# Graph-attention block on one core: probabilities times normalised tokens, head weights afterwards

## The chip, the core and the metric

The kernel runs on one core of a Trainium2 chip. The metric is the device time of one execution in microseconds, taken as the median of the runs shown. A core has TensorE (PE, matrix products into the accumulators called PSUM), VectorE (DVE), ScalarE (ACT), GpSimd (POOL) and SyncE (SP, which here only issues DMAs), and 16 DMA engines that they share. Each engine works through its own list of instructions in order and meets the others through semaphores.

## The reference, cut to what matters

There are 8 batches of 1024 tokens with 256 features and one adjacency matrix of 1024 x 1024. The first layer is a plain graph layer, the second a graph-attention layer with 4 heads, a second attention with one head over the joined heads, and a feed-forward network.

```python
h = jnp.maximum(_layernorm(x), 0.0)
x = x + deg[None, :, None] * (h @ Wi.T + b) + einsum('ij,bjo->bio', adj, h @ Wj.T)
h = jnp.maximum(_layernorm(x), 0.0)
# attention, for each head: Wh = h @ W[head], a logit for each pair of tokens from two vectors
Wh = jnp.einsum('bnf,hfo->bhno', h, W_heads)
e = f1[:, :, :, None] + f2[:, :, None, :]
e = jnp.where(adj > 0, leaky_relu(e, 0.01), -1e9)
attn = jax.nn.softmax(e, axis=-1)
head = jax.nn.elu(jnp.einsum('bhnm,bhmo->bhno', attn, Wh))
# heads joined: the same attention once more with W_out, elu, then
y = jnp.maximum(out @ w1 + b1, 0.0) @ w2 + b2 + out
x = x + layernorm(y) * gamma + beta
```

For a head, `attn @ (h @ W)` equals `(attn @ h) @ W`.

## The kernel before

Products of float32 quality are made from float16 parts: a value is split into a high and a low part, and three products (high-high, high-low, low-high) are added in PSUM. Such a split is made by ACT for the high part and by DVE for the low part, both reading the same source.

**Units and pairs.** The attention is cut into units of 128 rows of probabilities over 1024 columns. A batch has 32 units in layer 1 (4 heads x 8 row tiles) and 8 in layer 2; the 320 units run in a fixed order (lines 580 to 590): after the start, 32 units of layer 1 of one batch alternate with 8 units of layer 2 of the batch before. Two units are a pair. For each unit DVE adds logits and mask (`masked_row`, L941), ACT applies the leaky slope (L810), the exponential (L816) and the division (L823, `p_hi`), DVE makes `p_lo` (L948), POOL makes the small shift and the inverse of the sum (L742 to L757), and SP issues two transposes by DMA that bring the probabilities into `pt_hi` and `pt_lo` (L706, L708). There are 5 rows of logits (`X_SLOTS`), 2 of probabilities (`P_SLOTS`) and 4 of transposed ones (`T_SLOTS`). `attend` (L1166 to L1192) multiplies a pair by the values: 48 matmuls of 256 columns into psA. In layer 1 the values `val_hi` and `val_lo` are Wh, all four heads, and the result goes through elu (L829, L956, L962), a split (L837, L968) and `project` (L1194 to L1206, 12 matmuls of 258 columns with W_out into psD). After the fourth head of two row tiles ACT and DVE make `valo` (L842, L974) and `f12o` (L976), which are the values and logits of layer 2.

**The order.** Each engine runs one loop over steps n (from `START` to `STOP`); one unit enters per step, and a stage for unit k stands at step k plus its lag. The lags before: logits -5, leaky -4, exponential -3, `p_hi` -2, `p_lo` -1, transposes -1, `attend` +2, `elu_exp` +4, `elu` and `ht_high` +5, `ht_low` +6, `project` +7, `valo` +8. The step is only a position in each engine's list; engines drift apart as far as the semaphores and buffers let them.

**Side work.** Between the stages of the units stand the products that prepare the next batch and finish the one before. Their steps are fixed numbers relative to the first unit of the batch (`front(n, s)`, L645) or to the end of its layer 2 (`end2`): loading x (-46), its statistics and normalisation (-40 to -33), the graph products `z` and `d` (-32 to -27, two products of 16 matmuls of 512 columns each, twice), their eviction into `cat16` (L857, L1022), `x1` (-24 and -22, 48 matmuls of 256 columns each), the addition to xx (L1029), the second normalisation, `h1T` (-17 and -15, transposes on TensorE into PSUM, evicted as h1 by L862 and L1035), score rows (-12), their transpose (-10), storing and loading the logits (`save_f2`, `load_cat`), and `wh` (L1262 to L1267): one row tile of h1 times all four head weights, 12 matmuls of 512 columns, in each of the last 8 steps before the batch; for batch 1 all eight in one step. `wh` is evicted by `val_high` (L875) and `val_low` (L1046). The first pair of a batch waits for all eight (L1173). The feed-forward network (`ff1`, `ff2`, two halves) stands at +0, +2, +4, +6 after layer 2. All side products take turns on two PSUM buffers, psB and psC (`bank_task`, L617 to L625); each waits until the one two places earlier has been evicted (`open_bank`, L1208). `save_f2o` (L767) is a store of 1024 single elements into DRAM, issued by POOL 20 steps before `end2`.

Of the kernel before, what the change touches and what calls it, by code (L numbers as in the profile page):

```python
# [5 lines left out]
ALU = mybir.AluOpType  # L6
# [4 lines left out]
P = 128  # L11
# [9 lines left out]
VAL_SCALE = 2.0 ** (WH_LOG - LN_LOG - W_LOG)  # L21
CAT_LOG = 1
P_LOG = 15
VALO_SCALE = 2.0 ** (6 - WH_LOG - W_LOG)
X_SLOTS = 5
P_SLOTS = 2
T_SLOTS = 4


def build(nc, x, adj, w0, b0, w_heads, a_heads, w_out, a_out, w1, b1, w2, b2, gamma, beta, out):  # L30
# [12 lines left out]
    with ExitStack() as ctx:  # L43
# [44 lines left out]
        ff_half, y_half = big[:, 2, :], (big[:, 3, :], big[:, 0, :])  # L88
        o2T_half = tuple(big[:, i, :].rearrange("p (k n) -> p k n", k=KF) for i in range(2))
# [6 lines left out]
        h1_hi = hs_hi[:, :].rearrange("p (k n) -> p k n", k=KF)  # L96
        h1_lo = hs_lo[:, :].rearrange("p (k n) -> p k n", k=KF)
# [12 lines left out]
        h1hi_done, h1_done = sem("h1hi_done"), sem("h1_done")  # L110
# [23 lines left out]
        def scalar_stages(act, yy):  # L134
# [12 lines left out]
            def h1(s, k):  # L147
                act.wait_ge(h1_ps, s * 2 + k + 1)
                nc.scalar.activation(h1_hi[:, k, :], psD[:, :], ACT.Relu).then_inc(h1hi_done, 1)
            return h0, z_out, h1  # L150

        def vector_stages(dve, yy):
# [56 lines left out]
            def h1(s, k):  # L209
                dve.wait_ge(h1hi_done, s * 2 + k + 1)  # L210
                nc.vector.scalar_tensor_tensor(h1_lo[:, k, :], psD[:, :], 0.0, h1_hi[:, k, :], ALU.max, ALU.subtract).then_inc(h1_done, 1)
            return stats_of, means_of, normalise, h0, add_bias, z_out, x1, stats_x1, stats_x, h1
# [47 lines left out]
        with ExitStack() as tmp:  # L260
# [47 lines left out]
            with nc.Block() as block:  # L308
# [42 lines left out]
                def _(act):  # L351
                    h0, z_out, h1 = scalar_stages(act, yy)
# [19 lines left out]
                    h1(0, 0)  # L372
                    h1(0, 1)

                @block.vector
                def _(dve):
                    stats_of, means_of, normalise, h0, add_bias, z_out, x1, stats_x1, stats_x, h1 = vector_stages(dve, yy)
# [92 lines left out]
                    nc.vector.tensor_scalar(ebits[:, S_HINV:S_HINV + 1], kf[:, 0:1], -float(WH_LOG + P_LOG), None, ALU.add)  # L470
# [11 lines left out]
                    h1(0, 1)  # L482

# [46 lines left out]
        val_hi = sb("val_hi", [P, T, H, F], F16)  # L530
        val_lo = sb("val_lo", [P, T, H, F], F16)
# [20 lines left out]
        rows = yy[0:2 * H, :, :].rearrange("c t f -> c (t f)")  # L552
        stats_y = sb("stats_y", [P, T // 2, 6], F32)
# [14 lines left out]
        f1_done, rows_done, whhi_done, wh_done = sem("f1_done"), sem("rows_done"), sem("whhi_done"), sem("wh_done")  # L568
        x_in, x1_saved = sem("x_in"), sem("x1_saved")
        out_added = [sem(f"out_added_{i}") for i in range(2)]  # L570
        bank_full = [sem("psB_full"), sem("psC_full")]
# [778 lines left out]
```

## Time and profile before

| | |
|---|---|
| median of 3 runs | 1856.02 us (1854.7 to 1857.63) |
| the profiled execution's own time | 1850.8 us |
| its span | 1849.0 us |
| busy: PE / DVE / ACT / POOL | 1649.6 / 1473.5 / 1388.5 / 996.6 us |
| granted TensorE clock, mean | 0.957 |
| DMA, share of 16 engines (SP's queue) | 65.5% |

Busy time is the union of the instructions' durations on an engine. The end of a matmul is modelled and matmuls overlap, so for TensorE the distance between two starts says more than the duration. The granted clock is a share of the full 2.4 GHz.

### The profile page before, as it was taken

The page shows a single profiled execution, that of the slowest core. Times are in us where ns is not written, and L with a number is a line of the kernel's source. Part 1 is how long each engine was busy: PE and PEld are TensorE (multiplying, and loading weights), DVE is VectorE, ACT ScalarE, POOL GpSimd, SP SyncE. Part 2 cuts the span into 40 slices and gives each one's busy share as a digit, 9 for nine tenths or more (in the row PEclk, how much of TensorE's full clock was granted, in tenths as well). Part 3 has the DMA queues.
Part 4 walks back from the last instruction along what each step waited for, and adds up shares of the span by engine and source line. Part 5 has one row for each costly group of instructions (what it writes and reads, how often), then busy time and mean ns, then how long its engine had stood idle before and what let it go on. Part 6 is the DMA issues. An engine that isn't in the chain of part 4 may idle for free.

```text
span 1849.0 us, 34618 instructions
## 1 busy us (share of the span) xinstructions
PE 1649.6 (89%) x12568; PEld 1273.5 (69%) x12568; DVE 1473.5 (80%) x2459; ACT 1388.5 (75%) x1789; POOL 996.6 (54%) x1414
## 2 busy tenths in 40 slices
PE   6679979989999899898998899998998989988865
PEld 4437766678777777687676777677776876867653
DVE  5787876879887887978888798878879788788573
ACT  4078886879868797778886698687977789799560
POOL 2056653546465664746555565655646456586351
PEclk9789999999999999999999999999999999998988
DMA  6056783578757885759955897579856688589562
GB/s 222 25 122 106 138 178 57 109 102 160 157 90 117 132 177 102 110 102 140 176 98 97 119 161 145 91 112 133 176 102 105 104 140 158 101 145 134 101 97 42
DMA packets 713292, 225.57 MB, mean 122 GB/s; under 512 B 678784, under 2 KB 706432, under 8 KB 712992
## 3 DMA queue, kind: packets, MB, share of 16 engines
q1 hardware_dynamic: 704160, 214.92, 65.5%
q0 software_dynamic: 8960, 8.42, 3.9%
q8 instruction: 100, 1.64, 0.4%
q14 instruction: 72, 0.59, 0.1%
HBM read 38.54 MB, written 16.94 MB: 30 GB/s over the span
## 4 chain that ended last, share of the span: by engine, by line
PE 59%; DVE 15%; issue 6%; DMA 6%; ACT 4%; POOL 4%; SPq 1%; DVEq 0%; ACTq 0%; POOLq 0%
PE ps L1163 19%; PE ps L1191 10%; PE ps L1184 10%; PE ps L1185 10%; PE ps L1204 5%; DVE p_lo L948 3%; DMA pt_hi<-p_hi 3%; DVE xr L941 3%; PE ps L1283 2%; DMA pt_lo<-p_lo 2%; ACT xr L810 1%; ACT xr L816 1%; PE ps L1285 1%; ACT p_hi L823 1%; DVE stats_y L1058 1%
## 5 line engine op out<-in xcount | busy, mean ns | idle before, releaser
L1184 PE MATMUL ps<-pt_hi,val_hi 128*128 128x256 f16 x2048 | 474.8, 278 | 46.3 <-DMA pt_hi<-p_hi 27.7
L1185 PE MATMUL ps<-pt_hi,val_lo 128*128 128x256 f16 x2048 | 474.4, 278 | 0.0
L823 ACT ACTIVATE p_hi<-xr,rden 128x1024 f16<-128x1024 f32 x320 | 365.9, 1143 | 138.9 <-POOL rden L744 87.7
L948 DVE SCALAR_TENSOR_TENSOR p_lo<-xr,rden,p_hi 128x1024 f16<-128x1024 f32 x320 | 409.7, 1281 | 63.9 <-ACT p_hi L823 50.6
L742 POOL TENSOR_SCALAR den<-sums 128x1 f32<-128x1 f32 x320 | 165.5, 517 | 408.8 <-ACT xr L816 406.6
L816 ACT ACTIVATE xr<-xr,shift 128x1024 f32<-128x1024 f32 x320 | 365.4, 1142 | 0.0
L810 ACT ACTIVATE xr<-xr,f1h 128x1024 f32<-128x1024 f32 x256 | 292.5, 1143 | 64.4 <-DVE mx L941 63.9
L941 DVE CUSTOM_DVE_ANT_0 xr<-cat,mask_add 128x1024 f32<-128x1024 f32 x256 | 311.4, 1216 | 17.6 <-DMA cat<-f_rows 10.7
L755 POOL TENSOR_SCALAR zt<-mx,f1h 128x1 f32<-128x1 f32 x256 | 188.3, 736 | 227.8 <-DVE mx L941 224.8
L744 POOL TENSOR_TENSOR rden<-den,minus_one 128x1 f32<-128x1 f32 x320 | 284.2, 888 | 26.7
L1191 PE MATMUL ps<-pt_lo,val_hi 128*128 128x256 f16 x2048 | 271.5, 277 | 17.1 <-DMA pt_lo<-p_lo 17.0
L1184 PEld LDWEIGHTS ps<-pt_hi,val_hi 128*128 128x128 f16 x2048 | 203.9, 100 | 84.9 <-issue 32.1
L1191 PEld LDWEIGHTS ps<-pt_lo,val_hi 128*128 128x128 f16 x2048 | 202.7, 99 | 45.3 <-issue 19.1
L1185 PEld LDWEIGHTS ps<-pt_hi,val_lo 128*128 128x128 f16 x2048 | 204.0, 100 | 30.8 <-issue 2.6
L757 POOL TENSOR_SCALAR shift<-zt 128x1 f32<-128x1 f32 x320 | 180.0, 563 | 31.7
L1204 PE MATMUL ps<-wo_hi,ht_hi 128*128 128x258 f16 x512 | 144.4, 282 | 35.5 <-DVE ht_lo L968 21.6
L1204 PE MATMUL ps<-wo_hi,ht_lo 128*128 128x258 f16 x512 | 143.9, 281 | 0.0
L1204 PE MATMUL ps<-wo_lo,ht_hi 128*128 128x258 f16 x512 | 143.6, 280 | 0.0
L1184 PE MATMUL ps<-pt_hi,valo_hi 128*128 128x256 f16 x512 | 118.7, 278 | 8.5 <-DMA pt_hi<-p_hi 3.4
L1185 PE MATMUL ps<-pt_hi,valo_lo 128*128 128x256 f16 x512 | 118.7, 278 | 0.0
L829 ACT ACTIVATE eq<-ps,sc 128x512 f32<-128x512 f32 x160 | 107.7, 673 | 8.1 <-PE ps L1191 8.1
L1163 PE MATMUL ps<-adjT,hs_hi 128*128 128x512 f16 x224 | 90.3, 403 | 15.9 <-DVE big L1022 11.6
(195 smaller groups left out, 3066.7 us busy)
## 6 DMA issues: line engine op xcount, KB each, us to landing
cat<-f_rows SPq DMA_DIRECT2D x32, 512.0 KB, 4.9
out<-xx SPq DMA_DIRECT2D x32, 256.0 KB, 3.0
xx<-in_x SPq DMA_DIRECT2D x28, 256.0 KB, 4.7
out<-big POOLq DMA_DIRECT2D x28, 256.0 KB, 5.4
pt_hi<-p_hi SPq DMA_TRANSPOSE x320, 3.3
pt_lo<-p_lo SPq DMA_TRANSPOSE x320, 3.3
adj_i<-in_adj SPq DMA_DIRECT2D x4, 1024.0 KB, 10.6
f2o<-f2o_rows SPq DMA_DIRECT2D x8, 512.0 KB, 4.4
```

The source lines that it names most:

```text
L744: nc.gpsimd.tensor_tensor(rden[:, c], den[:, c], minus_one[:, :], ALU.pow).then_inc(rden_done, 1)
L755: nc.gpsimd.tensor_scalar(zt[:, c], mx[:, c], -1.0, f1, ALU.mult, ALU.subtract).then_inc(shift_half, 1)
L810: nc.scalar.activation(line, line, ACT.Prelu, bias=f1, alpha=ALPHA).then_inc(r_done, 1)
L816: nc.scalar.activation(line, line, ACT.Exp, bias=shift[:, k % 8:k % 8 + 1], accum_out=sums[:, k % 8:k % 8 + 1]).then_inc(p_done, 1)
L823: nc.scalar.activation(p_hi[:, k % P_SLOTS, :], xr[:, k % X_SLOTS, :], ACT.Copy, scale=rden[:, k % 8:k % 8 + 1]).then_inc(hi_done, 1)
L941: nc.vector.tensor_tensor_reduce(out=xr[:, k % X_SLOTS, :], in0=cat[:, m, :] if layer == 1 else f2o[:, :], in1=mask_row[:, tile, :], scale ...
L948: nc.vector.scalar_tensor_tensor(p_lo[:, k % P_SLOTS, :], xr[:, k % X_SLOTS, :], rden[:, k % 8:k % 8 + 1], p_hi[:, k % P_SLOTS, :], ALU.mu ...
L1163: last = nc.tensor.matmul(to, lhsT, rhs, start=i == 0, stop=i == len(pairs) - 1)
L1184: nc.tensor.matmul(to, vh, hi, start=t == 0, stop=False)
L1185: nc.tensor.matmul(to, vl, hi, start=False, stop=False)
L1191: last = nc.tensor.matmul(to, vh, pt_lo[:, slot:slot + 2, t * P:(t + 1) * P], start=False, stop=t == T - 1)
L1204: last = nc.tensor.matmul(psD[:, u * 512:u * 512 + V], h[:, c % 2, ft, tok], w[:, KF * m + ft, :], start=m == 0 and ft == 0 and g == 0, st ...
```

## The change

The values of layer 1 are no longer Wh. `attend` multiplies the probabilities by the normalised tokens h1 in token order (`hv_hi`, `hv_lo`, two batches' worth, 256 columns, the same for all heads). The result of a pair, `psA`, is split by ACT and DVE into `g_hi` and `g_lo`, and a new product `w_head` multiplies it by the head's weights into psC: 12 matmuls of 256 columns per pair. `elu` reads psC in layer 1 and psA in layer 2. `wh`, `val_high` and `val_low` are gone. The scales are adapted.

h1 in feature order is still needed for the score rows. It comes from `hv_hi` and `hv_lo` by four DMA transposes a batch, issued by SP (`turn_h1`), in place of `h1T` on TensorE. `hv` is split from the normalised tokens in SBUF. For batch 0 the setup makes both forms.

psC now belongs to `w_head`, so all side products share psB, each waiting for the eviction of the one before. The network's hidden part and its results get a buffer of their own (`fin`) in place of parts of `big` and `cat`. The order inside ACT's step changes, the lags grow (first lines of the diff), and the steps of the side work are written as tables, one for batch 1, one for the others.

```diff
+G_SCALE = 2.0 ** -P_LOG
+G_HIGH, G_LOW, W_HEAD = 3, 4, 4
+ELU_EXP, ELU, HT_HIGH, HT_LOW = 6, 7, 7, 8
+PROJECT, VALO_HIGH, VALO_LOW = 9, 10, 10
...
+        STEADY = dict(load_x=-52, x_stats0=-47, x_stats1=-45, x_rstd=-43, x_norm0=-42, h0_high0=-41, h0_low0=-39, h0_high1=-38,
+                      h0_low1=-35, z00=-32, z01=-32, d0=-30, z10=-26, z11=-26, d1=-24, cat_high0=-31, cat_high1=-27, cat_high2=-25,
+                      cat_high3=-23, cat_low0=-30, cat_low1=-26, cat_low2=-24, cat_low3=-22, x1_0=-21, x1_1=-20, x1_out0=-20,
+                      x1_out1=-18, save_x1=-18, x1_stats0=-18, x1_stats1=-17, x1_rstd=-16, x1_norm0=-13, hv_high0=-13, hv_low0=-12,
+                      x1_norm1=-12, hv_high1=-12, hv_low1=-12, turn0=-12, turn1=-12, rows=-10, rows_out=-9, f1T=-8, f1_out=-7,
+                      save_f2=-8, load_cat=-7)
+        SECOND = dict(load_x=-45, x_stats0=-40, x_stats1=-39, x_rstd=-38, x_norm0=-37, h0_high0=-36, h0_low0=-35, h0_high1=-34,
...
+        CLOSING = dict(ff1_0=0, ff2_0=3, ff1_1=3, ff2_1=5, hidden_0=1, hidden_1=4, y_0=3, y_1=7, save_f2o=-20, load_f2o=-16)
+        LAST = dict(ff1_0=2, ff2_0=2, ff1_1=4, ff2_1=6, hidden_0=1, hidden_1=5, y_0=3, y_1=7, save_f2o=-13, load_f2o=-12)
...
         def general(i):
-            return (psB, psC)[i]
+            return psB
...
+            def turn_h1(s, i):
+
+                half_of = slice(i * N, (i + 1) * N)
+                tiles = slice(i * half, (i + 1) * half)
+                for (whole, part), ready in (((hs_hi, hv_hi), h1hi_half), ((hs_lo, hv_lo), h1_half)):
+                    sp.wait_ge(ready, 2 * (s - 1) + i + 1)
+                    sp.dma_start_transpose(whole[:, half_of].rearrange("p (t i) -> p t i", t=T),
+                                           part[s % 2][:, tiles, :].rearrange("p t f -> p (t f)")).then_inc(h1T_in, DMA)
...
+            def g_high(j):
+
+                c = count1(j)
+                act.wait_ge(mm_done, j + 1)
+                if c >= 2:
+                    act.wait_ge(w_done, c - 1)
+                nc.scalar.activation(g_hi[:, c % 2, :, :].rearrange("p k n -> p (k n)"), psA[:, (j % 2) * 512:(j % 2 + 1) * 512], ACT.Copy,
+                                     scale=G_SCALE).then_inc(ghi_done, 1)
...
             for n in range(START, STOP):
-                if unit_at(n + 4) is not None:
-                    rectify(unit_at(n + 4))
-                if pair_at(n - 4) is not None:
-                    elu_exp(pair_at(n - 4))
...
+                j = pair_at(n - HT_HIGH)
+                if j is not None and kinds[2 * j][0] == 1:
+                    ht_high(j)
+                j = pair_at(n - G_HIGH)
+                if j is not None and kinds[2 * j][0] == 1:
+                    g_high(j)
...
+                if unit_at(n + 4) is not None:
+                    rectify(unit_at(n + 4))
                 if unit_at(n + 2) is not None:
                     high_part(unit_at(n + 2))
...
+            def g_low(j):
+                c = count1(j)
+                dve.wait_ge(ghi_done, c + 1)
+                nc.vector.scalar_tensor_tensor(g_lo[:, c % 2, :, :], psA[:, (j % 2) * 512:(j % 2 + 1) * 512].rearrange("p (k n) -> p k n", k=KF), G_SCALE,
+                                               g_hi[:, c % 2, :, :], ALU.mult, ALU.subtract).then_inc(g_done, 1)
...
-                if i == 0:
-                    pe.wait_ge(*((wh_done, T * (b + 1)) if layer == 1 else (valo_done, 4 * (b + 1))))
+                vals = (hv_hi[b % 2], hv_lo[b % 2]) if layer == 1 else (valo_hi[b % 2], valo_lo[b % 2])
+                if i == 0 and layer == 2:
+                    pe.wait_ge(valo_done, 4 * (b + 1))
+                if i == 0 and layer == 1 and b:
+                    pe.wait_ge(h1_half, 2 * b)
                 if j >= 2:
-                    pe.wait_ge(elu_done, j - 1)
+                    pe.wait_ge(*((g_done, count1(j - 2) + 1) if kinds[2 * j - 4][0] == 1 else (elu_done, j - 1)))
...
+            def w_head(j):
+
+                c, m = count1(j), head_of(2 * j)[2]
+                pe.wait_ge(g_done, c + 1)
+                if c >= 2:
+                    pe.wait_ge(elu_done, pair_of(c - 2) + 1)
+                to = pair_bank(j).rearrange("p (k n) -> p k n", k=KF)
+                for ft in range(KF):
+                    cols = slice(m * F + ft * P, m * F + (ft + 1) * P)
+                    for k in range(KF):
+                        for g, (v, w) in enumerate(three_g):
+                            last = nc.tensor.matmul(to[:, ft, :], w[:, k, cols], v[:, c % 2, k, :], start=k == 0 and g == 0, stop=k == KF - 1 and g == 2)
+                last.then_inc(w_done, 1)
...
                 if seq:
-                    pe.wait_ge(*emptied(*task_at[bank_task[name, s] - 2]))
+                    pe.wait_ge(*emptied(*task_at[bank_task[name, s] - 1]))
...
-            def wh(s, jt):
-                to, full = open_bank(f"wh{jt}", s)
-                tok = slice(jt * P, (jt + 1) * P)
-                for c in range(2):
-                    last = product(to[:, c * 512:(c + 1) * 512], [(h[:, k, tok], w[:, k, c * 512:(c + 1) * 512]) for k in range(KF) for h, w in three])
-                last.then_inc(full, 1)
```

## Rows read from the trace of the kernel before

**Rows 1.** The page's head and its busy time by engine.
```profile
span 1849.0 us, 34618 instructions
PE 1649.6 (89%) x12568; PEld 1273.5 (69%) x12568; DVE 1473.5 (80%) x2459; ACT 1388.5 (75%) x1789; POOL 996.6 (54%) x1414
```

**Rows 2.** Windows: one period; bounds, length, busy by engine, clock, DMA share, GB/s.
```profile
1134.30:1349.70 215.40, 201.88 (x1557) 156.82 (x1556) 179.18 (x294) 171.50 (x222) 123.98 (x176) 0.97 0.77 126
```

**Rows 3.** Chain of waits in order of time: start, length, runs of matmuls.
```profile
281.63 20.73 PE ps L1163 x96
...
1134.27 5.18 PE ps L1163 x24
...
1236.19 5.24 PE ps L1163 x48
```

**Rows 4.** Windows: ff1 of one half, then ff2 of one half.
```profile
1144.40:1147.90 3.50, 3.50 (x11) 1.54 (x10) 3.35 (x14) 1.41 (x3) 1.38 (x4) 1.00 0.56 109
1153.20:1158.40 5.20, 5.20 (x34) 4.79 (x33) 1.42 (x3) 5.18 (x7) 3.39 (x7) 1.00 0.65 126
```

**Rows 5.** Groups by line and shape: busy, mean ns of one, idle before.
```profile
L1046 DVE SCALAR_TENSOR_TENSOR val_lo<-ps,val_hi 128x1024 f16<-128x1024 f32 x64 | 77.9, 1217 | 21.9 <-ACT val_hi L875 21.9
...
L875 ACT ACTIVATE val_hi<-ps 128x1024 f16<-128x1024 f32 x64 | 64.8, 1012 | 51.5 <-PE ps L1163 51.4
...
L974 DVE SCALAR_TENSOR_TENSOR valo_lo<-ps,valo_hi 128x512 f16<-128x512 f32 x32 | 22.0, 688 | 72.5 <-ACT valo_hi L842 72.5
...
L842 ACT ACTIVATE valo_hi<-ps 128x512 f16<-128x512 f32 x32 | 18.8, 586 | 0.6 <-PE ps L1204 0.6
```

**Rows 6.** Timeline of ACT: start, duration; two neighbours.
```profile
1235.89 1.16 ACT L810 ACTIVATE xr<-xr,f1h 128x1024 f32<-128x1024 f32 x1
1236.93 1.16 ACT L816 ACTIVATE xr<-xr,shift 128x1024 f32<-128x1024 f32 x1
```

**Rows 7.** Windows: two stretches with idle PE, then five plain layer-1 pairs.
```profile
1187.00:1213.30 26.30, 21.82 (x133) 13.17 (x132) 24.56 (x40) 16.80 (x22) 19.00 (x24) 0.87 0.73 111
1255.30:1276.30 21.00, 13.60 (x122) 11.56 (x120) 17.76 (x39) 10.83 (x15) 12.52 (x18) 0.94 0.98 86
1627.50:1665.30 37.80, 34.21 (x300) 28.56 (x300) 34.03 (x48) 37.40 (x51) 29.87 (x41) 1.00 0.93 152
```

**Rows 8.** PE's waits, 463.2 to 1564.5: us in total, times, longest.
```profile
PE ps L1184 <- DMA pt_hi<-p_hi: 18.5, 4, 5.3
PE ps L1204 <- DVE ht_lo L968: 14.4, 7, 2.5
PE ps L1163 <- DVE big L1022: 11.6, 5, 3.6
PE ps L1191 <- DMA pt_lo<-p_lo: 8.5, 4, 6.6
PE ps L1184 <- DVE eq L962: 5.7, 5, 1.4
```

**Rows 9.** Timelines of POOL, then SP: start, duration of the issue.
```profile
1259.05 0.99 POOL L769 DMA_DIRECT2D f2o_rows<-f12o  x1
...
1258.31 1.23 SPq L708 DMA_TRANSPOSE pt_lo<-p_lo  x1
...
1260.26 1.68 SPq L706 DMA_TRANSPOSE pt_hi<-p_hi  x1
1264.51 6.66 SPq L708 DMA_TRANSPOSE pt_lo<-p_lo  x1
```

**Rows 10.** Timeline of PE: the first matmul of the first attention.
```profile
127.65 0.39 PE L1184 MATMUL ps<-pt_hi,val_hi 128*128 128x256 f16 x1 [7.44 <-DVE val_lo L1046]
```

**Rows 11.** Windows: the long stretches of the span, the third overlapping the second.
```profile
1559.50:1715.70 156.20, 141.72 (x1135) 115.94 (x1133) 131.03 (x197) 135.17 (x180) 104.10 (x146) 0.97 0.78 125
1715.70:1833.90 118.20, 88.34 (x568) 68.30 (x568) 60.04 (x107) 51.99 (x69) 39.12 (x59) 0.91 0.48 78
127.70:463.20 335.50, 308.65 (x2472) 242.30 (x2473) 271.56 (x420) 275.69 (x353) 189.57 (x271) 0.96 0.68 121
463.20:1564.50 1101.30, 1035.14 (x7998) 803.47 (x7997) 918.58 (x1495) 883.09 (x1139) 631.65 (x897) 0.97 0.75 126
```

More of the change, by code:

```diff
@@ L372, in _ @@
                     h1(0, 0)
+                    hv(0)
                     h1(0, 1)
@@ L623, in bank @@
+        START_TOO = ("rows", "rows_out", "f1T", "f1_out", "save_f2", "load_cat") + tuple(CLOSING)
+        opened = {"z0": "z00", "z1": "z10"}
+        order = sorted((step(opened.get(name, name), s), s, at, name) for s in range(B)
+                       for at, name in enumerate(FRONT + HEADS + FFN) if s or name not in FRONT)
+        bank_task = {(name, s): i for i, (_, s, _, name) in enumerate(order)}
         def bank(name, s):
-            return bank_task[name, s] % 2, bank_task[name, s] // 2
+            return 0, bank_task[name, s]
@@ L847, in h0_high @@
                 if i == 0:
-                    which, seq = bank(f"wh{T - 1}", s - 1)
+                    which, seq = bank("rows", s - 1)
                     act.wait_ge(bank_full[which], seq + 1)
@@ L893, in _ @@
                     softmax(unit_at(n + 3))
+                j = pair_at(n - HT_HIGH)
[4 more added lines that the diff above has]
+                    g_high(j)
+                for layer in (1, 2):
+                    j = pair_at(n - ELU_EXP + (0 if layer == 1 else 2))
+                    if j is not None and kinds[2 * j][0] == layer:
+                        elu_exp(j)
@@ L1085, in _ @@
             for n in range(START, STOP):
-                if pair_at(n - 5) is not None:
-                    elu(pair_at(n - 5))
+                j = pair_at(n - G_LOW)
+                if j is not None and kinds[2 * j][0] == 1:
+                    g_low(j)
+                for layer in (1, 2):
+                    j = pair_at(n - ELU + (0 if layer == 1 else 2))
+                    if j is not None and kinds[2 * j][0] == layer:
+                        elu(j)
                 if unit_at(n + 5) is not None:
@@ new lines, in _ @@
+                    if due(n, s, "h0_low1"):
+                        h0_low(s, 1)
+                        add_bias(s)
+                    for i in range(4):
+                        if due(n, s, f"cat_low{i}"):
+                            cat_low(s, i)
+                    for i in range(2):
+                        if due(n, s, f"x1_out{i}"):
+                            x1_out(s, i)
+                    if due(n, s, "x1_stats0"):
+                        moments1(0, s)
+                    if due(n, s, "x1_stats1"):
+                        moments1(1, s)
+                        means(ln1_stats, ln1_mv, s)
@@ L1181, in attend @@
                     for t in range(T):
-                        vh, vl = (val_hi[:, t, m, cols], val_lo[:, t, m, cols]) if layer == 1 else (valo_hi[b % 2][:, t, cols], valo_lo[b % 2][:, t, cols])
+                        vh, vl = vals[0][:, t, cols], vals[1][:, t, cols]
                         hi = pt_hi[:, slot:slot + 2, t * P:(t + 1) * P]
```

353 lines of the change are left out of this document (145 added, 208 removed).

## Prediction

> **What bounds the kernel now.** I read the page's busy shares first: TensorE (PE) 89%, VectorE (DVE) 80%, ScalarE (ACT) 75%; no engine is idle enough to be ignored [rows 1]. The kernel repeats itself every 40 steps (32 units of layer 1, 8 of layer 2), so next I cut the trace at equal points of that pattern: one period is 215.4 us, with PE busy 201.9, DVE 179.2, ACT 171.5 [rows 2]. Busy PE is not PE work, since matmul records overlap. The starts give the work: 48 matmuls of 256 columns go through in 5.24 us, 109 ns each, and 24 of 512 columns in 5.18, 216 ns each [rows 3]. The two halves of the feed-forward network cost 3.5 + 5.2 us each [rows 4]. A period then holds: attention 20 pairs x 48 x 0.109 = 104.6; projections 16 x 12 x 0.110 = 21.2; head products wh 96 x 0.216 = 20.7; z 64 x 0.216 = 13.8; x1 96 x 0.109 = 10.5; the diagonal part 1.8; feed-forward 17.4; transposes of h1 16 x 0.109 = 1.7; score rows and f1T 3.1. Sum 194.8 of 215.4: PE is the bound, and 20.6 us a period are lost.
>
> Where: in 1187.0 to 1213.3 PE is busy 21.8 of 26.3 with a granted clock of 0.87, in 1255.3 to 1276.3 only 13.6 of 21.0 at 0.94 [rows 7]. The list of PE's waits over five periods names what ends the idle time: pt_hi 18.5 us and pt_lo 8.5 (transposes by DMA), ht_low 14.4, the low part of cat 11.6 [rows 8]. The second place is the clearer one. POOL issues the scattered store of f2o_rows at 1259.05, and the two transposes issued at 1260.26 and 1264.51 crawl: SP's issue of the second takes 6.66 us instead of some 1.3 [rows 9]. PE has nothing else queued then and starves. I book about 10 us of the 20.6 to this collision (7.4 idle, the rest matmuls at the lower of the two clock levels, 1.2 GHz, into which PE fell after standing idle) and 9 to the first place.
>
> **PE work of the change.** wh (96 x 512 columns a batch) becomes w_head (16 pairs x 12 x 256 columns): 20.7 to 16 x 1.31 = 20.9 us. It needs twice the weight loads; I cost them at nothing, because the existing 256-column matmuls already carry one load each at 109 ns. The h1 transposes (1.7) leave PE. Period: 194.8 - 1.6 = 193.2. So the change removes next to no PE work; what it can win is the 20.6 us of loss.
>
> **ACT and DVE.** Eviction of val: 8 x 1.012 (ACT) and 8 x 1.217 (DVE). Eviction of g: 16 halves, like valo_hi at 0.586 and valo_lo at 0.688 [rows 5]. Back to back, ACT starts 1.04 us apart with durations of 1.16 [rows 6], so 0.11 of each is overlap (0.08 on DVE): ACT -7.2 + 7.6, DVE -9.1 + 9.7 a period, both under +1. hv evicts from SBUF what h1T evicted from PSUM, same size, taken as equal. Both engines stay 13 to 21 us below PE. But in a plain layer-1 stretch they are now close: 5 pairs took 37.8 us, 7.56 each, with ACT busy 37.4 of it and PE with work for 6.57 [rows 7]. After, PE has 6.57 + 1.31 = 7.88 and ACT 7.56 + 0.48 = 8.04. Idle PE there is filled with work that used to be a lump before each batch. That is the gain, and its limit.
>
> **Balance over the steps.** I laid these costs on the 40 steps in groups of four. After the change PE leads in steps 0 to 23 (21 to 23.6 us per group, except 4 to 7). In steps 24 to 39 ACT or DVE leads: the attention of layer 2 is 21.0 us for 8 steps, while ACT alone needs 8 x 3.2 = 25.6 for the rows; hv, its split and the second normalisation fall into steps 27 and 28. Excess over PE: 3 if only the whole stretch counts, 11 if every group of four does (4.5 of it in steps 4 to 7, where DVE has the bias, y and its rescaling). I take 7.
>
> **The collision.** save_f2o stays at the same step and save_x1 beside it, so it happens again. But x1, 2 x 5.24 us of PE work without a transpose in it, moves from steps 16 and 18 to 19 and 20, just behind it, with w_head beside. In the same stretch ACT and DVE have some 5 us per group of slack. Cover of 10.5 plus an attention against a stall of 9: I leave 1 us; without the cover it is 10.
>
> **SP and the h1 transposes.** Four more DMA transposes a period, each about 1.3 us of SP's issue [rows 9], and both halves stand in one step. SP waits there for the second hv_low, which waits for a normalisation and an eviction begun in the same step (some 4 us); behind it stand the transposes of the next unit, on which ACT's next p_hi and PE's next pair wait. This is in the stretch where ACT and DVE lead, so it shows. Bounds 0 (SP ahead) and 12 (one transpose queue held for a crawl as long as that of [rows 9]); nearest is 4 x 1.3 less the slack, I take 3.
>
> **One bank for side products.** z, d, x1, rows, f1T and the network now share one PSUM buffer in place of two, so each waits for the eviction of the one before. The steps leave an attention between them (5.24 us against an eviction pair of 0.9 + 1.1 plus queue), except ff2_0 and ff1_1 in one step: 2 us. Bounds over ten handovers: 0 and some 20 to 40. The Trainium skill speaks against this: "Perfetto Trace Analysis", section Optimizing Tensor Performance, says that independent matmul groups should rotate through PSUM banks so that an eviction overlaps the next group. By that rule the change gives something away at every handover; the trace of before, with two buffers, still shows 11.6 us of PE waiting for the low part of cat, so the rule has a footing here.
>
> w_head of a pair stands behind the next pair's attention; g_high and g_low (0.6 + 0.7 plus at most a step of queue) have 5.2 us or more. Cost 0; at worst 1.7 x 16 = 27 if both engines run late. PE's wait for elu before an attention (5.7 in five periods [rows 8]) goes, as g is read earlier.
>
> Period after: 193.2 + 7 + 1 + 3 + 2 = 206.2, or 8.8 less than 215.0 on average.
>
> **The whole span.**
> - Before the first attention: it starts at 127.65, held 7.4 us by val_lo [rows 10], behind eight wh of batch 0 that alternate with their evictions. Without them the first two rows, their transposes and a start near 115 remain, plus 2.6 for the split of 2048 columns that hv adds to the setup: 118, so -9.7.
> - 127.7 to 463.2 [rows 11]: PE work 298 of 335.5. wh of batch 1, 20.7 us in one lump [rows 3], goes with the waits around it (about 11). After: work 308 plus 18: -9.5.
> - 463.2 to 1564.5, 5.12 periods [rows 11]: -45.
> - 1559.5 to 1715.7, the last layer-1 pass [rows 11]: 16 x 7.88 + 17.4 = 143.5 of PE work where 130 was, plus 10: -3.
> - The end [rows 11]: the longer way from attention to valo, and save_f2o one step later: +4 (bounds 0 and 8).
>
> Sum -63: span 1849.0 - 63 = 1786; the profiled run took 1850.8, 1.8 beyond its span: 1788. The median of the runs shown is 5.2 above that run: **1793**. Its own range is 1760 to 1825.
>
> **Rivals.**
> - *Everything hides.* The buffers carry PE over the weak stretch, period 199: 7.2 less over some 7 period lengths, -50: 1743. For it: PE runs 125 us without a long gap in 1134 to 1260. Against it: ACT would have to make up steps 32 to 39.
> - *The loss only moves.* The collision is not covered and SP's hold costs 6 to 8: period 213 to 216; the start and the lump of batch 1 remain as gain: about 1840.
> - *Slower: the single bank.* PE stands at each of ten handovers of psB until cat_low, x1_out or y_out has been through DVE's in-order queue. Each us per handover costs 10 x 7 = 70. It decides from 0.9 us on (63 / 70); with 1.5 it is 1793 + 105 = 1898. This is the case that the skill's rule would predict. For it: DVE is 83% busy and a side eviction stands last in its step. Against it: the steps between.
>
> **Chances.** Forecast 0.58; all hides 0.16; loss only moves 0.13; single bank 0.13. A run of this kernel can be told from no change by about 0.2%. Faster 0.84, same 0.03, slower 0.13 follow. The range 1738 to 1852 leaves out the slower case and the far end of the best.
>
> **What would show it.** A period of 206 us between equal points; w_head at 1.31 us a pair; no PE gap over 2 us beside the scattered store, though a transpose still takes 6 us or more there; the largest PE waits on transposes in steps 28 to 34, and SP held at the h1 transposes; 2 us at ff1_1. First attention near 118. It is wrong if PE waits on cat_low, x1_out or y_out add up to over 9 us a period, or if w_head waits for g_low in most pairs.

## The result and the profile after

| | before | after |
|---|---|---|
| median of 4 runs each | 1856.6 us (1854.7 to 1857.63) | **1753.58 us** (1749.39 to 1757.03) |
| ratio, 95% interval | 1 | **0.9445** [0.9421, 0.9469] |
| span of the profiled execution | 1849.0 us | 1753.4 us |
| granted clock, mean | 0.957 | 0.972 |
| busy PE / DVE / ACT | 89 / 80 / 75% | 91 / 84 / 80% |

The kernel became 103 us faster where 63 were forecast: the direction held, the size did not, and the time lies between the forecast's own range and the rival in which everything hides (1743). Chips differ: the unchanged kernel before took 1846.4 to 1856.6 us in the four comparisons of this study. So the times below are compared by their ratios. Periods are read from one profile each; the kernel after gave 200.4 and 200.2 us in two comparisons.

The page's head after, to be held against [rows 1]; busy time by engine:

```profile
span 1753.4 us, 36311 instructions
...
PE 1600.1 (91%) x13224; PEld 1323.0 (75%) x13224; DVE 1479.5 (84%) x2524; ACT 1395.3 (80%) x1854; POOL 1011.4 (58%) x1414
```

DVE and ACT did 6 and 7 us more than before: their work did not shrink, they wait less. The windows of the kernel after (bounds, length, busy PE, weight loads, DVE, ACT, POOL, clock, DMA share, GB/s) are one period (against [rows 2]), its stretch around the scattered store, five plain pairs and the weakest stretch ([rows 7]), then the second and the last long stretch ([rows 11]):

```profile
1065.40:1266.70 201.30, 194.97 (x1636) 162.40 (x1636) 179.50 (x302) 172.37 (x230) 127.23 (x175) 1.00 0.81 141
1170.00:1192.00 22.00, 22.00 (x204) 19.68 (x202) 15.74 (x24) 16.07 (x22) 9.88 (x19) 1.00 0.69 95
1197.70:1237.30 39.60, 39.60 (x351) 33.78 (x350) 37.70 (x58) 38.20 (x53) 29.71 (x38) 1.00 1.02 200
1240.00:1270.00 30.00, 24.94 (x222) 21.15 (x221) 27.12 (x53) 25.89 (x36) 20.06 (x29) 1.00 0.98 183
126.40:441.00 314.60, 305.71 (x2665) 256.49 (x2664) 270.75 (x425) 272.74 (x364) 185.30 (x263) 0.99 0.76 136
1467.80:1753.40 285.60, 236.61 (x1826) 196.03 (x1824) 202.04 (x333) 192.97 (x261) 144.28 (x206) 0.93 0.68 106
```

The reader is to see three things. A period is 201.3 us instead of 215.4, with DVE and ACT as busy as before. In five plain pairs PE never stands: 39.6 us, 7.9 a pair, the rate of its own work. And of the 6.3 us that are left idle in a period, 5 stand in a stretch like that of the fourth row, where layer 2's attention runs; the rest is one wait of 1.3 us at `ff1_1`.

PE's waits over five periods, against [rows 8] (us in total, times, longest):

```profile
PE ps L1218 <- DMA pt_hi<-p_hi: 9.5, 7, 2.0
PE ps L1194 <- DVE fin L1091: 6.6, 5, 1.3
PE ps L1218 <- DVE fin L1008: 5.3, 6, 0.9
PE ps L1251 <- DVE ht_lo L1014: 4.5, 6, 1.6
PE ps L1238 <- DVE g_lo L995: 1.2, 1, 1.2
PE ps L1224 <- DMA pt_lo<-p_lo: 0.5, 1, 0.5
```

The 11.6 us for the low part of cat are gone, transposes fell from 27.0 to 10.0, and `ht_low` from 14.4 to 4.5. The wait for elu (L1008) stayed: 5.3 against 5.7. Over the same five periods, before and after, the windows are:

```profile
487.20:1559.50 1072.30, 1006.14 (x7782) 782.20 (x7780) 895.73 (x1466) 857.16 (x1107) 617.29 (x875) 0.97 0.75 125
```
```profile
465.70:1467.80 1002.10, 974.56 (x8180) 812.13 (x8180) 893.72 (x1486) 861.98 (x1146) 628.83 (x873) 1.00 0.80 139
```

So a period has 7.7 us less of idle PE (13.2 to 5.5) and 6.3 us less of busy PE (201.2 to 194.9). Where the time of the span came from, between equal points of both profiles:

| stretch | before | after | difference | forecast |
|---|---|---|---|---|
| up to the first attention | 127.7 | 126.4 | -1.3 | -9.7 |
| to layer 2's first attention | 335.5 | 314.6 | -20.9 | -9.5 |
| five periods and what lies between the points | 1096.3 | 1026.8 | -69.5 | -45 |
| from the last batch's first probabilities to the end | 289.5 | 285.6 | -3.9 | +1 |
| **span** | 1849.0 | 1753.4 | **-95.6** | -63 |

The periods, from the start of one batch's first `p_hi` to the next, were 212.1, 215.2, 214.9, 215.4 and 214.8 us before (mean 214.5), and 199.8, 199.9, 200.0, 201.4 and 201.1 after (mean 200.4). The experiments are read by this mean.

### The profile page after: what moved, and what is told of

Same layout as the page of the kernel before. It is cut to its first block, busy times and chain, and to the rows that moved or that the text cites. A ratio compares the mean times of both kernels' runs of the same rounds, so it can differ in the third digit from the quotient of the medians.

```text
span 1753.4 us, 36311 instructions
## 1 busy us (share of the span) xinstructions
PE 1600.1 (91%) x13224; PEld 1323.0 (75%) x13224; DVE 1479.5 (84%) x2524; ACT 1395.3 (80%) x1854; POOL 1011.4 (58%) x1414
## 4 chain that ended last, share of the span: by engine, by line
PE 49%; DVE 15%; ACT 11%; DMA 8%; issue 8%; SPq 3%; POOL 2%; ACTq 0%; DVEq 0%; POOLq 0%
PE ps L1194 12%; PE ps L1224 8%; PE ps L1218 8%; PE ps L1219 8%; PE ps L1238 4%; DVE p_lo L989 4%; PE ps L1251 4%; ACT xr L858 3%; DMA pt_lo<-p_lo 3%; PE ps L1316 3%; DVE xr L982 3%; DMA pt_hi<-p_hi 3%; ACT xr L864 2%; ACT p_hi L871 2%; PE ps L1318 1%
## 5 line engine op out<-in xcount | busy, mean ns | idle before, releaser
L1218 PE MATMUL ps<-pt_hi,hv_hi 128*128 128x256 f16 x2048 | 463.8, 274 | 1.2 <-DMA pt_hi<-p_hi 1.1
L1219 PE MATMUL ps<-pt_hi,hv_lo 128*128 128x256 f16 x2048 | 464.0, 274 | 0.0
L1224 PE MATMUL ps<-pt_lo,hv_hi 128*128 128x256 f16 x2048 | 266.7, 273 | 8.7 <-DMA pt_lo<-p_lo 8.7
L808 POOL TENSOR_SCALAR shift<-zt 128x1 f32<-128x1 f32 x320 | 239.4, 748 | 31.7
L1224 PEld LDWEIGHTS ps<-pt_lo,hv_hi 128*128 128x128 f16 x2048 | 200.9, 98 | 33.3 <-issue 9.4
L1218 PEld LDWEIGHTS ps<-pt_hi,hv_hi 128*128 128x128 f16 x2048 | 201.0, 98 | 29.8 <-issue 5.5
L1219 PEld LDWEIGHTS ps<-pt_hi,hv_lo 128*128 128x128 f16 x2048 | 200.9, 98 | 27.9 <-issue 4.0
L1251 PE MATMUL ps<-wo_hi,ht_hi 128*128 128x258 f16 x512 | 140.6, 275 | 10.4 <-DVE ht_lo L1014 10.4
L1238 PE MATMUL ps<-g_hi,wh_hi 128*128 128x256 f16 x512 | 139.6, 273 | 2.9 <-DVE g_lo L995 2.9
L1238 PE MATMUL ps<-g_lo,wh_hi 128*128 128x256 f16 x512 | 139.6, 273 | 0.0
L1238 PE MATMUL ps<-g_hi,wh_lo 128*128 128x256 f16 x512 | 139.6, 273 | 0.0
```

The lines of the kernel that those rows point to most:

```text
L808: nc.gpsimd.tensor_scalar(shift[:, c], zt[:, c], ALPHA, zt[:, c], ALU.mult, ALU.min).then_inc(shift_done, 1)
L1218: nc.tensor.matmul(to, vh, hi, start=t == 0, stop=False)
L1219: nc.tensor.matmul(to, vl, hi, start=False, stop=False)
L1224: last = nc.tensor.matmul(to, vals[0][:, t, cols], pt_lo[:, slot:slot + 2, t * P:(t + 1) * P], start=False, stop=t == T - 1)
L1238: last = nc.tensor.matmul(to[:, ft, :], w[:, k, cols], v[:, c % 2, k, :], start=k == 0 and g == 0, stop=k == KF - 1 and g == 2)
L1251: last = nc.tensor.matmul(psD[:, u * 512:u * 512 + V], h[:, c % 2, ft, tok], w[:, KF * m + ft, :], start=m == 0 and ft == 0 and g == 0, st ...
```

## The experiments

The questions behind them: how much of the gain is the collision with the scattered store, covered by the products that now lie around it; whether the rest belongs to the new algebra, to the new steps, or to both only together; what the single bank costs; and what bounds the kernel now.

**1. The collision taken away, in both kernels.** f2o is stored as 128 runs of 64 bytes in place of 1024 single elements. What this changes in the computation: layer 2 reads its column logits in another order.

```diff
-pool.dma_start(f2o_rows[b:b + 1, :].rearrange("b (t p) -> p (b t)", p=P), f12o[b % 2][:, :, 1],
+pool.dma_start(f2o_rows[b:b + 1, :].rearrange("b (p u) -> p (b u)", p=P), f12o[b % 2][:, :, :].rearrange("p t c -> p (t c)"),
```

In the kernel before:

> The kernel before, but the store of f2o_rows writes both columns of f12o as 128 runs of 64 bytes instead of 1024 single elements; layer 2 then reads logits in a wrong order. Theory (cover): each period of the kernel before loses about 10 us because the scattered store makes two transposes crawl while PE has nothing else queued; without the crawl the period falls from 215 to about 205 and the time by 60 to 75 us, to about 1790. Rival (balance): the collision plays little, the gain of the change came from wh spread over the pairs; then this kernel stays within 15 us of 1856.

Measured: 1808.89 us, 0.9797 [0.9779, 0.9815], period 209.2. One period of it:

```profile
1107.80:1316.40 208.60, 199.02 (x1558) 154.82 (x1556) 178.64 (x294) 171.48 (x223) 127.39 (x175) 0.99 0.71 130
```

The store cost 5.3 us a period, 38 in all, not the 10 a period that I had booked. The time lies between the two expectations. The gap of 5.6 us (start to start) is gone, and PE still idles for 9.6 us of that period without any scattered store. The gain stands where the store is: from the attention at 1047.3 us of the kernel before, 3 us behind a store, to the one at 1077.0 the same work takes 5.1 us less, and the same 5.1 less in `b_store17` below.

In the kernel after:

> The changed kernel with the same store in 64-byte runs (layer 2 reads logits in a wrong order). Theory (cover): the crawl is already hidden behind x1 and w_head, so taking it away gives 0 to 8 us, 1746 to 1754. Rival (balance): the crawl costs the changed kernel as much as before, so some 60 us go, to about 1695.

Measured: 1739.24 us, 0.9411 [0.9396, 0.9426], period 200.2 against 200.4. In the steady periods the store costs nothing any more; the gain of about half a per cent against the unaltered kernel lies after the last batch's start (285.6 to 272.4 us). There no x1 of a next batch stands behind the store. In the kernel after the store at 1564.26 us leaves PE this wait, and with the long runs it is gone:

```profile
1577.16 1.23 PE L1224 MATMUL ps<-pt_lo,hv_hi 128*128 128x256 f16 x5 [7.92 <-DMA pt_lo<-p_lo]
```

**2. The store moved, scattered as it was.** In the kernel before it is moved to step 17, between the two halves of x1; in the kernel after from step 20, between them, to step 22, behind them.

```diff
-                    if at == (-20 if s < B - 1 else -14):
+                    if at == (-23 if s < B - 1 else -14):
```
```diff
-        CLOSING = dict(... save_f2o=-20, load_f2o=-16)
+        CLOSING = dict(... save_f2o=-18, load_f2o=-16)
```

> The kernel before with save_f2o issued three steps earlier (step 17 of the batch, between the two halves of x1, as it stands in the changed kernel). Nothing else moved. Theory (cover): the second half of x1 (5.2 us) and an attention whose operands are there lie beside the crawl; period about 207 to 209, time 1800 to 1820. Rival (balance): within 10 us of 1856.

Measured: 1819.49 us, 0.9851 [0.9836, 0.9866], period 209.9. Moving it under x1 wins nearly all that taking it away wins. The transposes still crawl: those issued at 1219.07 and 1220.61 us, behind a store at 1216.77, land after 11.7 and 10.4 us, and no wait of PE over 1.1 us follows in the next 40 us.

> The changed kernel with save_f2o issued two steps later (step 22), where PE has only attentions, w_head and projections left. Theory (cover): the crawl shows up as PE idle time, 5 to 9 us a period and lower clock after it; time 1795 to 1820. Rival (balance): no change, 1750 to 1760.

Measured: 1771.38 us, 0.9583 [0.9566, 0.9599], period 203.4. Right in direction, only 3.0 us a period where 5 to 9 were expected. The distances from attention to attention agree with those of the kernel after to 0.02 us, except in the eight pairs that follow the store. A period of it, then its waits over five periods:

```profile
1283.40:1486.40 203.00, 195.51 (x1636) 162.24 (x1636) 176.21 (x282) 172.06 (x231) 125.23 (x173) 1.00 0.80 132
```
```profile
PE ps L1218 <- DMA pt_hi<-p_hi: 11.1, 11, 2.2
PE ps L1251 <- DVE ht_lo L1014: 8.5, 8, 1.6
```

Together: cover is shown in the kernel before, where the crawl stays and its cost goes. The same store at another step costs 0 to 5 us a period. In the kernel after the step decides too (0.2 against 3.0), but there x1 does a second thing, which the prediction did not have: it stands ahead of the next attention in PE's list, so the slots for transposed rows come free late, and SP issues nothing from 1176.4 to 1182.23 us, when the attention behind x1 has ended. The store at 1174.16 then catches one transpose, that of 1174.08. The profile has no landing for it, but DVE's `p_lo`, which overwrites its source, waits for it until 1186.70, some 12 us after its issue:

```profile
1186.70 1.28 DVE L989 SCALAR_TENSOR_TENSOR p_lo<-xr,rden,p_hi 128x1024 f16<-128x1024 f32 x1 [2.05 <-DMA pt_lo<-p_lo]
```

**3. The new algebra with the old steps.** For batches 2 to 7 the table is filled with the steps of the kernel before.

```diff
-STEADY = dict(load_x=-52, x_stats0=-47, ... z00=-32, z01=-32, d0=-30, z10=-26, z11=-26, d1=-24, ... x1_0=-21, x1_1=-20,
+STEADY = dict(load_x=-46, x_stats0=-40, ... z00=-32, z01=-31, d0=-30, z10=-29, z11=-28, d1=-27, ... x1_0=-24, x1_1=-22,
```

> The changed kernel, but its table of steps for batches 2 to 7 (STEADY) carries the step numbers of the kernel before: z at -32 to -28, x1 at -24 and -22, the first normalisation packed into -40 to -33; everything else (g, w_head, one bank, DMA transposes of h1, lags) stays changed. The collision was worth 6 us a period, 8.5 of the 14.5 won per period are open. Theory A (the tables): side work packed close together on DVE and PE makes those 8.5, so the period goes to 209 or more, with one bank instead of two perhaps 215, time 1815 to 1850. Theory B (the algebra: wh spread over the pairs, psA free earlier): the period stays at 200.5 plus at most the 6 of the collision, time 1755 to 1795.

Measured: 1860.41 us, 1.007 [1.0055, 1.0085], period 219.3. Slower than the kernel before by 0.7%. The first theory's "209 or more" holds for the period, but its time (up to 1850) and the whole of the second theory are missed. A period, then the waits:

```profile
1136.20:1354.50 218.30, 199.50 (x1639) 163.73 (x1638) 179.77 (x302) 172.57 (x231) 123.66 (x175) 0.98 0.75 129
```
```profile
PE ps L1218 <- DMA pt_hi<-p_hi: 39.1, 17, 5.5
PE ps L1194 <- DVE big L1068: 22.0, 14, 2.4
PE ps L1238 <- DVE g_lo L995: 12.0, 5, 2.7
PE ps L1224 <- DMA pt_lo<-p_lo: 9.2, 1, 9.2
```

Three things are back: the uncovered store (in each of the five periods one wait behind it, 9.2 us for `pt_lo` and four of 5.0 to 5.5 for `pt_hi`, 30 us together), the wait for the low part of cat (L1068), now on one bank, and a good 18 us of other waits for `pt_hi`, which the kernel before did not have.

**4. The old algebra with the new steps.** The same steps were put into the kernel before, for the same batches, with `wh` left in its eight steps and the first part of h0 two steps later; the core of it:

```diff
-                        if at == -28:
+                        if at == (-28 if s < 2 else -26):
...
-                        if n == START + u if s == 0 else at == -21 + u:
+                        if n == START + u if s == 0 else at == (-21 if s == 1 else -18) + u:
```

> The kernel before (Wh as values, two banks, wh in the last eight steps, h1T on TensorE) with the new steps for the side work of batches 2 to 7 as far as its parts exist: statistics at -47 and -45, z at -32 and -26, x1 at -21 and -20, the h1 transposes at -13 and -12; the first part of h0 stays two steps later than in the new table, since h0 waits for the last wh. Theory A (the tables make the gain, whatever the algebra): period 203 to 206, time 1770 to 1800. Theory C (tables and algebra need each other: wh keeps PE full around the batch change and holds h0 back): 209 to 215 a period, 1810 or more.

Measured: 1817.48 us, 0.981 [0.979, 0.9829], period 208.1, between the ranges of the two theories (203 to 206, 209 to 215). A period, then its waits:

```profile
1107.80:1316.10 208.30, 198.55 (x1558) 154.71 (x1557) 179.19 (x294) 171.33 (x223) 123.45 (x175) 0.99 0.73 130
```
```profile
PE ps L1204 <- DVE ht_lo L968: 15.2, 15, 2.0
PE ps L1163 <- DVE hs_lo L1035: 13.8, 5, 2.8
PE ps L1184 <- DVE eq L962: 10.6, 10, 1.8
PE ps L1244 <- DVE yy L1003: 7.7, 5, 1.6
PE ps L1184 <- DMA pt_hi<-p_hi: 2.5, 6, 1.1
```

Nearly all waits for transposes are gone (27.0 to 2.5 us, 4.9 a period): x1 now stands behind the store here too. What is left waits for DVE: for the split of h1 out of the PSUM bank, for `ht_low`, and for elu before an attention. PE's waits in the kernel after are 4.4 us a period less than these, and its work 1.6 less; the two are most of the 7.7 between the kernels. Which part of the change removes which wait, no run shows.

The mean period, us:

| | old steps | new steps |
|---|---|---|
| old algebra | 214.5 | 208.1 |
| new algebra | 219.3 | 200.4 |

"New algebra" stands here for all of the change but the steps of batches 2 to 7: the lags, ACT's order, the single bank, `fin` and the transposes of h1 by DMA go with it, and no run parts them. Neither part alone makes the gain. The steps bring -6.4 with the old algebra, most of it the store that is now covered, and -18.9 with the new; the algebra +4.8 with the old steps and -7.7 with the new.

**5. The single bank under pressure.** Only z, d and their evictions stand on the old steps, all else as in the kernel after.

```diff
-h0_low1=-35, z00=-32, z01=-32, d0=-30, z10=-26, z11=-26, d1=-24, cat_high0=-31, cat_high1=-27, ...
+h0_low1=-35, z00=-32, z01=-31, d0=-30, z10=-29, z11=-28, d1=-27, cat_high0=-30, cat_high1=-29, ...
```

> The changed kernel with only z, d and their evictions at the old steps (z -32, -31, -29, -28, d -30, -27), all the rest of the new table. The old table cost 18 us a period on the changed kernel. If the handovers of the single bank carry it: 6 to 9 us a period, 1800 to 1820. If the packed normalisation ahead of z carries it: under 3 us a period, up to 1775.

Measured: 1782.18 us, 0.9625 [0.9611, 0.9639], period 204.7, between the two expectations. The wait that answers to `cat`, over five periods:

```profile
PE ps L1194 <- DVE big L1068: 17.8, 14, 2.3
```

17.8 us in five periods are 3.6 of the 4.3 us that the period grew. On the old steps the products stand one behind the other, one to a step; on the new ones two or four steps lie between z and d, so that the eviction of one is over before the next wants the bank. The steps between the products, not a second bank, are what keeps this wait away in the kernel after. Of the 18.9 us that the old steps cost, these 4.3 are shown to be z, d and the bank, and the waits behind the uncovered store are 6.0. The rest was not taken apart by a run; in the trace PE was granted the lower level for 61.4 us of the five periods of experiment 3, and for none of the kernel after. At half the rate that is up to 6 us a period, an estimate.

**6. Less PE work.** `w_head` gets 8 matmuls a pair in place of 12; left out is the product of `g_hi` with the low part of the weights.

```diff
-            three_g = [(g_hi, wh_hi), (g_hi, wh_lo), (g_lo, wh_hi)]
+            three_g = [(g_hi, wh_hi), (g_lo, wh_hi)]
```

> The changed kernel without the product of g_hi with the low part of the head weights: 8 matmuls per pair instead of 12 in w_head, 7 us of PE work less per period (the output loses precision). If PE alone bounds layer 1: 7 us a period, 50 to 56 in all, 1700. If ACT is close behind, as its 8.04 us of work per plain pair against PE's 7.88 says: a third to two thirds of it, 1715 to 1735.

Measured: 1733.98 us, 0.9388 [0.9374, 0.9402], period 197.5. A period, then the waits over five:

```profile
1052.80:1251.90 199.10, 190.17 (x1572) 156.30 (x1572) 179.43 (x302) 172.15 (x231) 126.33 (x176) 0.99 0.80 141
```
```profile
PE ps L1251 <- DVE ht_lo L1014: 11.5, 12, 1.6
PE ps L1218 <- DMA pt_hi<-p_hi: 10.2, 9, 1.9
PE ps L1238 <- DVE g_lo L995: 6.7, 5, 2.2
```

PE's work falls by 64 x 0.109 = 7.0 us a period, the period by 2.9, which is the expected third to two thirds. In plain pairs PE is the bound: from attention to attention they take 7.44 us in place of 7.87, less by the four matmuls that were left out. In the last pairs of the period, around layer 2's attention, most of it is given back: there `ht_lo` and `g_lo` come late as soon as PE is quicker.

**7. The start.** For batch 1 the early side work stands two to three steps later, so that the first attention comes ahead of it in PE's list.

```diff
-SECOND = dict(load_x=-45, x_stats0=-40, x_stats1=-39, ... z00=-31, z01=-29, d0=-29, ...
+SECOND = dict(load_x=-45, x_stats0=-37, x_stats1=-36, ... z00=-29, z01=-28, d0=-27, ...
```

> The changed kernel with the table for batch 1 (SECOND) moved two to three steps later up to x1, so that the first rows of batch 0 and the first attention stand ahead of batch 1's statistics and of its first z. Theory: PE's wait of 27 us for hs_lo ahead of the first attention, and DVE's of 10.8 for x, are why the start brought 1.3 us and not 9.7; the first attention comes near 118 and the time falls by 4 to 9 us, to 1745 to 1750. Rival: the loads of the logits, not the order, set the first rows, and nothing is won.

Measured: 1755.01 us, 0.9505 [0.9491, 0.9519]. The first attention starts at 123.3 us, 3 us earlier than in the profile of the kernel after (126.4) and 1 us earlier than in that of `a_again` (124.3), and the first batch takes 161.2 us instead of 157.7: nothing is won. Its row on PE:

```profile
123.30 0.37 PE L1218 MATMUL ps<-pt_hi,hv_hi 128*128 128x256 f16 x1 [29.61 <-DMA pt_hi<-p_hi]
```

**8. The feed-forward's second half one step later.** `ff1_1`, `hidden_1` and `ff2_1` move to 4, 5 and 6, so that `ff1_1` no longer stands in one step with `ff2_0`.

```diff
-CLOSING = dict(ff1_0=0, ff2_0=3, ff1_1=3, ff2_1=5, hidden_0=1, hidden_1=4, ...
+CLOSING = dict(ff1_0=0, ff2_0=3, ff1_1=4, ff2_1=6, hidden_0=1, hidden_1=5, ...
```

> The changed kernel with the second half of the network one step later (ff1_1 4, hidden_1 5, ff2_1 6), so that an attention and a w_head lie between ff2_0 and ff1_1, which share the bank. Theory: the 1.6 us PE gap ahead of ff1_1 goes in seven periods, 8 to 11 us, to about 1744. Rival: y_out and the rescaling come later on DVE's list and give it back, within 3 us of 1754.

Measured: 1752.5 us, 0.9484 [0.9468, 0.95], period 199.2. The period falls by 1.2 as the handover is freed, but the end grows by 4.0 us (289.6), and the sum is nothing where 8 to 11 us were expected. That no other work fills the step at the end is my reading; experiment 9 keeps the end as it was.

**9. The kernel after once more, and a better one.** The unaltered kernel after, on the same chip as 4, 5 and the next:

> The changed kernel unaltered, as the reference for the others on this chip: ratio 0.9445 as before, within 0.3%.

Measured: 1752.48 us (1751.29 to 1754.67), 0.9466 [0.9451, 0.948]. Then the move of 8, for the batches 0 to 5 alone:

```diff
+        LATER = dict(ff1_1=4, hidden_1=5, ff2_1=6)
...
+                if s < B - 2 and name in LATER:
+                    return end2[s] + LATER[name]
```

> The changed kernel with the network's second half one step later for batches 0 to 5 only, so that the end of the kernel keeps its steps (in a_ff the period fell by 0.9 us and the end grew by 4). 0.9 x 6 = 5 us, 0.3%, below a_again; rival: nothing.

Measured: **1747.81 us** (1747.53 to 1748.79), 0.9441 [0.9425, 0.9456], period 199.1. It is 0.27% below the kernel after on its chip, with ranges that do not touch, and so the fastest kernel of the study that leaves nothing out.

## Why the prediction was right in direction and short in size

**PE's work: right.** `w_head` was to take what a pair of `wh` took, and no weight load to be seen. The pair pitch of 7.9 us in the plain stretch is the 6.57 + 1.31 of the forecast, with PE at work throughout.

**ACT and DVE: right.** The groups after, by line and shape (busy, mean ns, idle before):

```profile
L1238 PE MATMUL ps<-g_hi,wh_hi 128*128 128x256 f16 x512 | 139.6, 273 | 2.9 <-DVE g_lo L995 2.9
...
L995 DVE SCALAR_TENSOR_TENSOR g_lo<-ps,g_hi 128x512 f16<-128x512 f32 x128 | 87.4, 683 | 31.7 <-ACT g_hi L879 31.7
...
L879 ACT ACTIVATE g_hi<-ps 128x512 f16<-128x512 f32 x128 | 75.1, 587 | 62.6 <-PE ps L1224 62.5
```

`g_hi` 587 ns against 586 and `g_lo` 683 against 688 from [rows 5]. `w_head` waited 2.9 us for `g_lo` in the whole execution, as the prediction's zero had it.

**Balance over the steps: nearly right in size.** PE's gaps in the stretch of layer 2's attention add up to 1.1 + 1.8 + 1.0 + 1.3 + 1.2 = 6.4 us in a period from start to start, or 5.9 without the 0.11 that each matmul takes anyway (7 forecast). Two of the five wait for elu (L1008), a wait that the prediction let go: it holds for layer 1 alone, as layer 2's elu still reads psA. One of their releasers, on ACT, and the wait at `ff1_1`, on PE:

```profile
1256.45 0.69 ACT L886 ACTIVATE eq<-ps,sc 128x512 f32<-128x512 f32 x1 [3.15 <-DVE ht_lo L1014]
```
```profile
1086.79 0.70 PE L1194 MATMUL ps<-fin,w_sb 128*128 128x512 f32 x1 [1.32 <-DVE fin L1091]
```

The second is the handover of the single bank that I put at 2 us; 1.6 were measured from start to start, 1.5 of them loss. Experiment 8 confirms it: freed, the period falls by 1.2.

**The single bank as a rival: not here.** PE's waits on evictions of the other side products over five periods are none at all for cat and x1. The Trainium skill, "Perfetto Trace Analysis", section Optimizing Tensor Performance, says to rotate groups through banks so that evictions overlap the next group. The runs agree with the rule only where the products follow each other within a step or two: 3.6 us a period in experiment 5, 4.4 in experiment 3, and 0 in the kernel after. Two banks with the old steps still waited 2.3 us a period (11.6 in five).

**The collision: mis-sized.** The prediction booked 10 us of the old period to it; experiment 1 gives 5.3, and 4.6 by experiment 2. Of the 7.4 us idle in the second row of [rows 7], 5.3 wait for the transpose; the other 2.1 are waits for elu and for `ht_low`, which I had booked to the collision too. It left 1 us after the change; it was 0.2. That a crawl stays and x1 covers it was right; that x1 also holds SP's next transposes back was not foreseen. POOL's store and SP's transposes beside it, after, against [rows 9]:

```profile
1174.16 0.99 POOL L820 DMA_DIRECT2D f2o_rows<-f12o  x1
```
```profile
1172.76 1.23 SPq L752 DMA_TRANSPOSE pt_hi<-p_hi  x1
1174.08 2.32 SPq L754 DMA_TRANSPOSE pt_lo<-p_lo  x1
1182.23 1.23 SPq L752 DMA_TRANSPOSE pt_hi<-p_hi  x1
1183.50 3.52 SPq L754 DMA_TRANSPOSE pt_lo<-p_lo  x1
```

The longest issue takes 3.5 us there in place of 6.66, and PE is busy for 22.0 of 22 us beside it. Where no x1 follows, in the last batch, the forecast had no cost for the store; it was 7.9 us of waiting.

**SP and the h1 transposes: mis-sized, 3 us forecast and nothing found.** SP's waits over five periods:

```profile
SPq L751 <- PE ps L1224: 186.6, 50, 8.3
...
SPq L717 <- DVE xx L1075: 1.4, 3, 0.6
SPq L742 <- ACT hv_hi L918: 0.3, 1, 0.3
```

SP stands 0.3 us for `hv_hi` and not at all for the low part, and 186.6 us, 37 a period, for PE to free the slots of transposed rows. It runs ahead of PE, which was the condition of the lower bound, and that was the right end.

**The stretch 127.7 to 463.2: mis-sized.** The forecast kept 18 us of loss beside 308 of work. The window after is 314.6 us: 6.6 of loss by the same sum. PE runs through it at a clock of 0.99, 305.7 us busy, and idles 8.9 us where it idled 26.9. The lump of `wh` and its handovers are gone, as forecast; what the forecast left out is the first store, behind which PE waited 7.4 us at 413 us of the kernel before. Experiment 1 alone shortens this stretch from 335.5 to 330.0 us.

**The period: mis-sized as their sum.** 206.2 forecast, 200.4 measured. Of the 5.8 us, 3 are SP's hold, 1.1 the balance, 0.8 the collision and 0.5 the bank; the last 0.4 is less than the periods differ among themselves (199.8 to 201.4). What I had not seen is where the other loss of the old period went: 14.1 us were won, of which 1.6 is PE's work and 5.3 the collision. The rest, 7.2, is by the traces the first stretch of [rows 7], with its waits for `ht_low` (2.5 us) and for the low part of cat (2.0 us), and the clock (no run took these apart): 0.97 in [rows 2], 1.00 after. In the five periods PE was granted the lower level for 58.0 us before, and never after; from 130 us to the end of the last attention for 113.1 us before and 34.1 after. It fell there after PE had stood idle; fewer and shorter gaps give back the gap and the slow matmuls behind it. The two windows above say it in sizes: of the 14.1 us, 7.7 are idle time and 6.3 busy time, and of the 6.3 only 1.6 is work. The other 4.7 fit the 11.6 us a period at half the rate, up to 5.8, an estimate. So the forecast kept the idle time of the parts that it thought untouched, and with them their share of the slow clock.

**The start: the step that failed.** "Without them the first two rows, their transposes and a start near 115 remain", with 2.6 added for the longer setup 118: 126.35 was measured, 1.3 us earlier in place of 9.7. Three rows on DVE and one on PE:

```profile
84.31 2.28 DVE L223 SCALAR_TENSOR_TENSOR hv_lo<-yy_first,hv_hi 128x2048 f16<-128x2048 f32 x1
...
97.38 1.41 DVE L1029 BATCH_NORM_STATS2 stats<-xx 128x6 f32<-128x256 f32 x4 [10.79 <-DMA xx<-in_x]
...
119.41 1.21 DVE L1055 SCALAR_TENSOR_TENSOR hs_lo<-yy,hs_hi 128x1024 f16<-128x1024 f32 x1
```
```profile
120.77 0.59 PE L1194 MATMUL ps<-adjT,hs_hi 128*128 128x512 f16 x1 [27.21 <-DVE hs_lo L1055]
```

In PE's list a product of batch 1 stands ahead of the first attention, and waits 27 us for a split which DVE reaches only after the first rows. Behind it stood a second limit, which experiment 7 lays bare: with that product moved away, the first attention waits for `pt_hi` and starts at 123.3. It needs the logits back from DRAM, the rows of a pair on three engines and two transposes, and that chain is the same in both kernels (the first `p_hi` starts at 112.6 before and 112.1 after). The `wh` that I took for the bound lay beside it. The wait of 7.4 us in [rows 10] named the last releaser, not the time at which all others were ready.

**The chances.** "Everything hides" had 0.16, for a period of 199 and a time of 1743; the measured period is 1.4 above it, and the version of experiment 9 gets to 199.1. The time is 11 us from that rival and 39 from the forecast, so the rival had the better number, but not for its reason: the weak stretch still costs 5.9 us of the 7 that it said would be hidden. Its argument that PE runs without a long gap from 1134 to 1260 us did not hold either; waits of 2.5 and 2.0 us stand there, in the first stretch of [rows 7].

## What to carry to other kernels

A stall at a fixed step can be cured by work that lies behind it in the list of the engine that would wait: the same scattered store costs 0 or 5 us a period, by its step alone. The order alone brought 6.4 us and the new algebra alone lost 4.8, and together they brought 14, so neither can be priced with the other held at its old value. When a lump goes, price the gaps around it at the lower clock too; and when an early wait goes, follow the next releaser in the list: the first matmul's time is set by the latest of them.

## What the runs showed of the hardware

- A store of 1024 single elements slows transposes that are under way. In the kernel before the issue of one took SP 6.66 us in place of 1.3 [rows 9], and the slowest landings were 12.1 and 10.1 us. The tiles `pt_hi`, then `pt_lo`, from 1240 to 1280 us in the kernel before:

```profile
DMA to landing us min/median/max: 3.2/3.3/12.1
...
DMA to landing us min/median/max: 3.0/3.3/10.1
```

  With 128 runs of 64 bytes in its place (experiment 1) most transpose issues around it took 1.2 to 1.9 us and the longest 2.4.
- The time at the lower clock level fell from 58.0 us to 0 in the five periods, with PE's work down by only 1.6 us in each. The gaps that remain, of 1.0 to 1.8 us each, left the granted clock of the period at 1.00.
- Twice as many weight loads (`w_head` against `wh`) cost nothing visible: 39.6 us for five pairs, PE busy throughout; four of its matmuls fewer made a pair 0.44 us shorter, 0.109 each.
